# One more of the 16 states weighted on VectorE in half of the scan's tiles, and one product over two PSUM banks

## The chip, the cores and the metric

The kernel runs on one NeuronCore of a Trainium2 chip. The metric is the device time of one launch in microseconds. Before the change the median of three runs is 2026.62 us (2025.83 to 2028.26).

## The reference, cut to what matters

Input x is 4 sequences of 1024 tokens, 256 features, float32. Four stages follow one another, each added to x: latent attention, a spiking feed-forward layer, a selective scan, and the feed-forward layer again. The change is in the scan alone, which computes for each feature d and each of 16 states n:

```
A_tilde = exp(dt[..., None] * A)                    # A = -exp(A_log)
B_tilde = where(|A| < 1e-8, dt, (A_tilde - 1) / (A + 1e-10))
h   = A_t * h + B_t * Bp_t[:, None, :] * u_t[:, :, None]     # over time
y_t = einsum('bn,bdn->bd', Cp_t, h)
y = (y + u * D_param) * silu(z);   return y @ W_out.T
```

## The kernel before, in words

`scan` puts features on partitions (256 features are two halves, f = 0 and 1) and time on the free axis. Time is cut into 8 tiles of 512 tokens; a sequence is two tiles. Tiles 0, 2, 4 and 6 begin a sequence, so their recurrence starts from zero; tiles 1, 3, 5 and 7 take an incoming state. In each tile a loop over n = 0..15 takes one state at a time, "a unit" g = 16 t + n, all five engines in program order with semaphores between them; there is no scheduler, the order is the order of the code.

One unit goes through these steps:

- SyncE loads B and C of the state, spread over the partitions, into `bc` (L1556).
- GpSimd multiplies u by B into `ring` (`make_input`, L1574, 128x1024), three units ahead of the unit that it weighs next.
- ScalarE makes the decay exp(dt a) for each half in the PSUM pair `a_bank[g % 2]` (L1780). As there are two pairs, decay g waits until unit g-2 has left its pair: until it is scanned, and, if VectorE weighs unit g-2, until it has been weighed and its last column saved.
- VectorE forms (a - 1) x in `ring` (`scale`, L1895), then the recurrence (`run`, L1904), for each half.
- The result is multiplied by C ("weighted") into `outs`, 128x1024: on GpSimd (L1582) for most units, on VectorE (`weigh`, L1912) for the units that `on_dve` names. For those, the recurrence is written back into `a_bank` rather than `ring`.
- In tiles that begin a sequence ScalarE copies the last column into `state` (`keep_state`, L1794), right before decay g if unit g-2 is weighted on VectorE, right behind it otherwise.
- TensorE adds the unit into two PSUM banks `y_bank` with a diagonal matrix (L1639), three units late.

Work for other tiles is laid between the units. On ScalarE: at n = 6, 8, 9, 10, 11 and 12 pieces of the next tile's softplus and of its u (at n = 10 a table load, two logarithms and a second table load, L1756, L1759, L1741; at n = 8 and 12 a table load, silu and a table load), at n = 14 silu(z) of half 0 between two table loads (L1738, L1741), and half 1 at n = 0 of the next tile. On VectorE: `gate` (L1872) at n = 2 multiplies the previous tile's two y banks by silu(z), one 128x512 product each, a residual add at n = 3 and n = 15, and `soft`, three products, behind n = 11 and behind n = 12.

VectorE's order around a unit: scale(g, half 1), then weigh(g-1) if it is VectorE's, run(g, half 0), scale(g+1, half 0), run(g, half 1), then the extras of that n.

Of the kernel before, what the change touches and what calls it, by code (L numbers as in the profile page):

```python
# [6 lines left out]
F32 = mybir.dt.float32  # L7
BF16 = mybir.dt.bfloat16
I32 = mybir.dt.int32
ALU = mybir.AluOpType  # L10
# [3 lines left out]
P = 128  # L14
B, S, D = 4, 1024, 256
T = B * S
TW = 512
NT = T // TW
TPB = S // TW
DC = D // P  # L20
# [10 lines left out]
NS = 16  # L31
# [1433 lines left out]
def scan(nc, io, x, xn, xn_scr, w, begun, bc_scr, next_loads, xn_next):  # L1465
# [8 lines left out]
    OUTS = 5  # L1474
    AHEAD = 3
    LAG = 3
    D_UNIT = 8
    ON_DVE, ON_DVE_LAST = (3, 7, 11), (3, 6, 9, 12, 15)
    with ExitStack() as ctx:
        m = Mem(nc, ctx)  # L1480
        wz, wout, wtap, wpar, wdt, b_dt = (w[n] for n in ("wz", "wout", "wtap", "wpar", "wdt", "b_dt"))
        a_col, is_small = w["decay"][:, 1], w["decay"][:, 2]
        d_diag, rec_diag, ones, small_int, par, dt, bc = (begun[n] for n in (
            "d_diag", "rec_diag", "ones", "small_int", "par", "dt", "bc"))
        u = [begun["u0"], m.sb("u1", [P, DC, TW])]
        state = m.sb("state", [P, DC, NS])
        e_part, relu_part, log_part = (m.sb(n, [P, DC, TW]) for n in ("e_part", "relu_part", "log_part"))
        sz = m.sb("sz", [P, 2, DC, TW])
        gy = m.sb("gy", [P, DC, TW])
        ring = m.sb("ring", [P, RING, DC, TW])  # L1490
        outs = m.sb("outs", [P, OUTS, DC, TW])
        small_part = m.sb("small_part", [P, TW])
        norm = TokenNorm(m, x, w["ident"], "_nx", e_part[:].rearrange("p c (j d) -> p (c j) d", d=D))
        a_bank = [m.ctx.enter_context(nc.psum_tensor(f"a_bank{i}", [P, DC, TW], F32)) for i in range(2)]
        y_bank = [m.bank(f"ys_bank{f}") for f in range(DC)]
        w0, w1 = m.bank("work0"), m.bank("work1")

        decay_set, taps_set, diag_set, bc_out_done, bc_in = (begun[n] for n in (
# [22 lines left out]
            return (t + 1) // TPB * NS + (n if t % TPB == 0 else 0)  # L1521

        def on_dve(g):
            return g % NS in (ON_DVE if g // NS < NT - 1 else ON_DVE_LAST)

        def weighted_by(g):

            mine = on_dve(g)
            return (dve_weighted if mine else weighted), sum(on_dve(k) == mine for k in range(g + 1))
# [30 lines left out]
        def _(pool):  # L1560
# [26 lines left out]
            for g in range(UNITS):  # L1587
                if g + AHEAD < UNITS:
                    make_input(g + AHEAD)
                if not on_dve(g):  # L1590
                    weigh(g)

        @block.tensor
        def _(pe):
# [27 lines left out]
                product(bank, [(wz[:, c, f * P:(f + 1) * P], xn_of(t, c)) for c in range(DC)], z_made)  # L1622

            def out(t, i, bank):
                pe.wait_ge(gated, DC * t + DC)
                for b in (2 * i, 2 * i + 1):
                    for f in range(DC):
                        mm = nc.tensor.matmul(bank[:, b % 2 * D:(b % 2 + 1) * D], gy[:, f, b * P:(b + 1) * P], wout[:, f],
                                              start=(f == 0), stop=(f == DC - 1))
                mm.then_inc(out_made, 1)  # L1630

            def unit_sum(g):
                t, n = g // NS, g % NS
                if n == 0:

                    pe.wait_ge(gated, DC * t)
                pe.wait_ge(*weighted_by(g))
                for f in range(DC):
                    mm = nc.tensor.matmul(y_bank[f][:], rec_diag[:, f * NS + n], outs[:, g % OUTS, f],  # L1639
                                          start=(n == 0), stop=(n == NS - 1))  # L1640
                    if n == D_UNIT and f == 0:
                        for k in range(DC):
                            nc.tensor.matmul(y_bank[k][:], d_diag[:, k], u[t % 2][:, k], start=False, stop=False)
                mm.then_inc(summed, 1)

            pe.wait_ge(diag_set, 1)
# [2 lines left out]
            for t in range(NT):  # L1649
                more = t + 1 < NT  # L1650
                for n in range(NS):
                    if t >= TPB and n == 2:

                        pe.wait_ge(z_kept, DC * t)
                        out(t - 2, 1, w1)
# [37 lines left out]
                    if t and more and n == 15:  # L1693

                        pe.wait_ge(soft_made, DC * (t + 2))
                        out(t - 1, 0, w0)
                    if not more and n == 5:

                        pe.wait_ge(x_new, 2 * (t - 1))
                        out(t - 1, 0, w0)  # L1700
# [6 lines left out]
                    if t * NS + n >= LAG:  # L1707
                        unit_sum(t * NS + n - LAG)
            for g in range(UNITS - LAG, UNITS):
                unit_sum(g)  # L1710
# [5 lines left out]
        def _(act):  # L1716
# [16 lines left out]
            def silu_z(t, f, bank):  # L1733
                act.wait_ge(z_made, DC * t + f + 1)
                if t >= 2:

                    act.wait_ge(gated, DC * (t - 1))
                nc.scalar.activation(sz[:, t % 2, f], bank, ACT.Silu).then_inc(z_kept, 1)  # L1738

            def exp_tables():  # L1740
# [55 lines left out]
            for t in range(NT):  # L1796
                more = t + 1 < NT
                for n in range(NS):
                    g = t * NS + n
# [5 lines left out]
                    if t and n == 0:  # L1805
                        silu_z(t - 1, 1, w1[:])
                        exp_tables()
# [30 lines left out]
                    if n == 14:  # L1838
                        silu_z(t, 0, w1[:])
                        exp_tables()  # L1840
                    if not more and n == 15:
                        silu_z(t, 1, w1[:])
                        exp_tables()
# [4 lines left out]
        def _(dve):  # L1848
# [16 lines left out]
            def gate(t):  # L1865
                dve.wait_ge(summed, NS * t + NS)
                dve.wait_ge(z_kept, DC * t + DC)
                if t:

                    dve.wait_ge(out_made, DC * t)  # L1870
                for f in range(DC):
                    nc.vector.tensor_tensor(gy[:, f], y_bank[f][:], sz[:, t % 2, f], ALU.mult).then_inc(gated, 1)  # L1872

            def add(t, i, bank):
                dve.wait_ge(out_made, 2 * t + i + 1)
# [42 lines left out]
            def tiles(with_small):  # L1918
                scale(0, 0, with_small)
                for t in range(NT):  # L1920
                    more = t + 1 < NT
                    for n in range(NS):
                        g = t * NS + n
                        scale(g, 1, with_small)
                        if g and on_dve(g - 1):
                            weigh(g - 1)
                        run(g, 0)
                        if g + 1 < UNITS:
                            scale(g + 1, 0, with_small)
                        run(g, 1)  # L1930
                        if t and n == 2:
                            gate(t - 1)
                        if t >= TPB and n == 3:
                            add(t - 2, 1, w1)
                        if more and n == 11:
                            soft(t + 1, 0, w0[:])
                        if more and n == 12:
                            soft(t + 1, 1, w0[:])
                        if t and more and n == 15:
                            add(t - 1, 0, w0)  # L1940
                        if not more and n == 5:
                            add(t - 1, 0, w0)
                        if not more and n == 6:
                            add(t - 1, 1, w1)
                        if not more and n == 4:
                            norm.statistics(nc, dve, 0, 0)
                        if not more and n == 7:
                            norm.finish(nc, dve, 0)
# [5 lines left out]
            if on_dve(UNITS - 1):  # L1954
                weigh(UNITS - 1)
            gate(NT - 1)
            add(NT - 1, 0, w0)
            add(NT - 1, 1, w1)
# [35 lines left out]
def program(nc, io, out):  # L1994
# [5 lines left out]
    with ExitStack() as ctx:  # L2000
# [8 lines left out]
        with ExitStack() as second:  # L2009
            m = Mem(nc, second)  # L2010
            xn_scan = m.sb("xn_s", [P, XN, DC, TAPS - 1 + TW])
            w, loads = scan_weights(m, io)
            wpr_last = m.sb("wpr_f2", [P, FC, D])
            ident = w["ident"]
            with ExitStack() as feed:
                given = feed_weights(Mem(nc, feed), io, "_f1")
                merge_heads(nc, io, x, o_scr, recip_scr, early, given[2], ident, given[3])
                merging.close()
                begun = first_scan_tile(m)
                feed_forward(nc, x, "_f1", given[:3], ident, io=io, xn_scan=xn_scan, xn_scr=xn_scr, more_loads=loads, w=w,  # L2020
                             begun=begun, bc_scr=bc_scr)
            wfc_last = w["wtap"][:].rearrange("p k c d -> p (k c d)").rearrange("p (c f) -> p c f", c=DC)

            def xn_next(c):
                return xn_scan[:, (NT + 1) % XN, c, 0:TW]

            scan(nc, io, x, xn_scan, xn_scr, w, begun, bc_scr,
                 ((wfc_last, io["W_fcT"].rearrange("(c p) f -> p c f", p=P)),
                  (wpr_last[:], io["W_projT"].rearrange("(f p) d -> p f d", p=P))), xn_next)
            xn_last = m.sb("xn_f2", [P, 2, DC, TW])  # L2030
            feed_forward(nc, x, "_f2", (wfc_last, wpr_last, xn_last), ident, out=out, xn_first=xn_next)
# [13 lines left out]
```

## Time and profile before

| what | value |
|---|---|
| median of three runs | 2026.62 us |
| the profiled execution | 2029.69 us, span 2027.7 us |
| TensorE granted clock, mean | 0.957 |
| busy, share of the span | PE 92%, DVE 80%, ACT 54%, POOL 34% |
| the scan, VectorE's first to last instruction | about 1240.7 to 1792.9 us of the span |

PE is TensorE, DVE VectorE, ACT ScalarE, POOL GpSimd, SP SyncE; PEld is TensorE's weight load. The shares of the whole span mix four stages, so the scan has to be read from its own stretch. A row of the trace gives start, duration, engine, line, operation, and in brackets how long that engine sat idle before it and what ended the wait. Durations of neighbouring VectorE rows overlap by about 0.1 us; start-to-start distances are what an instruction costs.

### The profile page before, as it was taken

What the parts mean: (1) busy time and instruction counts of PE and PEld (TensorE: products, weight loads), DVE (VectorE), ACT (ScalarE), POOL (GpSimd) and SP (SyncE); (2) the same over time, 40 slices, a digit from 0 to 9 for tenths busy, and PEclk for the clock granted to TensorE, in tenths of its full rate; (3) what the DMA queues carried; (4) which work ended last, traced back from release to release, by engine and by line L of the source; (5) the groups of instructions that cost most, each with busy time, mean ns of one, the idle gap of its engine ahead of it and who ended that gap; (6) DMA issues with size and microseconds to landing.
All of it is one profiled execution on the core that took longest, in us unless ns stands there. A gap on an engine that the chain in (4) does not pass through costs nothing. (4 is left out here: it accounts for less than half of the span.)

```text
span 2027.7 us, 25794 instructions
## 1 busy us (share of the span) xinstructions
PE 1868.1 (92%) x7414; PEld 826.8 (41%) x7414; DVE 1625.9 (80%) x2596; ACT 1087.7 (54%) x1511; POOL 697.9 (34%) x474
## 2 busy tenths in 40 slices
PE   7898999999999999999999997798889877789998
PEld 4441332332322322323676663333333333356665
DVE  6878998998998988974556666999999999955654
ACT  5552665666665666674244335766576657333321
POOL 3561000001100000010000015999999999800000
PEclk9996998999998999999999997899999999899999
DMA  4850222122221122203210003455545545400000
GB/s 134 175 129 13 62 51 42 45 43 44 46 45 44 43 48 38 48 12 122 82 42 21 22 23 118 126 143 136 135 121 142 137 122 164 99 6 16 22 21 21
DMA packets 100394, 147.13 MB, mean 73 GB/s; under 512 B 15089, under 2 KB 54401, under 8 KB 98721
## 3 DMA queue, kind: packets, MB, share of 16 engines
q1 hardware_dynamic: 100256, 145.42, 28.6%
q8 instruction: 72, 1.18, 0.3%
q14 instruction: 66, 0.53, 0.1%
HBM read 114.69 MB, written 30.29 MB: 71 GB/s over the span
## 5 line engine op out<-in xcount | busy, mean ns | idle before, releaser
L840 DVE TENSOR_REDUCE mx<-max_bank 128x1 f32<-128x512 f32 x960 | 618.1, 687 | 65.0 <-PE max_bank L749 64.7
L826 ACT ACTIVATE probs<-score_bank 128x1024 f32<-128x1024 f32 x512 | 496.9, 1021 | 289.7 <-PE score_bank L763 288.8
L749 PE MATMUL max_bank<-ks,qs 96*128 96x512 bf16 x960 | 336.0, 390 | 0.0
L763 PE MATMUL score_bank<-qs,ks 99*128 99x512 bf16 x1024 | 313.6, 388 | 14.5 <-issue 10.4
L1639 PE MATMUL ys_bank<-outs,rec_diag 128*128 128x512 f32 x512 | 260.2, 642 | 67.3 <-POOL outs L1582 43.5
L1574 POOL TENSOR_TENSOR ring<-u,bc 128x1024 f32<-128x1024 f32 x128 | 300.6, 2359 | 0.4 <-DMA bc<-bc_scr 0.3
L809 PE MATMUL o_bank<-probs,vg 128*32 128x512 f32 x2048 | 275.5, 610 | 0.5 <-ACT probs L826 0.5
L1780 ACT ACTIVATE a_bank<-dt,decay_s 128x512 f32<-128x512 f32 x256 | 170.7, 686 | 150.5 <-DVE ring L1904 98.1
L1582 POOL TENSOR_TENSOR outs<-ring,bc 128x1024 f32<-128x1024 f32 x102 | 239.9, 2352 | 13.6 <-DVE ring L1904 13.6
L1252 PE MATMUL y_bank_f<-wpr_f,hid_f 128*128 128x256 f32 x1024 | 236.4, 379 | 0.0
L703 POOL CAST neg_parts<-neg_max 16x128 bf16<-16x128 f32 x31 | 8.7, 282 | 639.1 <-DVE neg_max L853 639.1
L1252 PEld LDWEIGHTS y_bank_f<-wpr_f,hid_f 128*128 128x128 f32 x1024 | 193.4, 190 | 59.9 <-issue 38.3
L1324 ACT ACTIVATE relu_f<-hid_bank_f 128x512 f32<-128x512 f32 x128 | 76.3, 596 | 250.9 <-PE hid_bank_f L1243 225.3
L749 PEld LDWEIGHTS max_bank<-ks,qs 96*128 96x128 bf16 x960 | 94.1, 98 | 281.1 <-DVE mx L840 187.1
L1895 DVE SCALAR_TENSOR_TENSOR ring<-a_bank,ring 128x512 f32<-128x512 f32 x256 | 172.6, 674 | 22.5 <-ACT a_bank L1780 21.6
L1639 PEld LDWEIGHTS ys_bank<-outs,rec_diag 128*128 128x128 f32 x512 | 99.3, 202 | 207.6 <-issue 114.9
L1414 DVE SCALAR_TENSOR_TENSOR hid_f<-hid_bank_f,relu_f 128x512 f32<-128x512 f32 x128 | 86.9, 688 | 97.0 <-ACT relu_f L1324 95.2
L763 PEld LDWEIGHTS score_bank<-qs,ks 99*128 99x128 bf16 x1024 | 99.6, 100 | 123.1 <-issue 27.4
L1904 DVE TENSOR_TENSOR_SCAN ring<-a_bank,state,ring 128x512 f32<-128x512 f32 x100 | 127.8, 1278 | 0.0
L1904 DVE TENSOR_TENSOR_SCAN ring<-a_bank,ring 128x512 f32<-128x512 f32 x104 | 126.3, 1214 | 0.0
L1243 PE MATMUL hid_bank_f<-xn_f,wfc_f 128*128 128x512 f32 x256 | 116.5, 592 | 1.1 <-PEq L972 1.1
L1613 PE MATMUL work<-xn_s,wtap_s 128*128 128x512 f32 x224 | 107.0, 616 | 7.3 <-DVE x L1876 7.3
(233 smaller groups left out, 1933.7 us busy)
## 6 DMA issues: line engine op xcount, KB each, us to landing
bc<-bc_scr SPq DMA_DIRECT2D x128, 512.0 KB, 5.0
qk_parts<-parts SPq DMA_DIRECT2D x128, 96.0 KB, 1.9
qs<-qk_parts SPq DMA_DIRECT2D x128, 64.0 KB, 4.3
o_scr<-o_sb SPq DMA_DIRECT2D x32, 256.0 KB, 2.0
ks<-qk_parts SPq DMA_DIRECT2D x16, 384.0 KB, 4.7
xn_s<-xn_scr SPq DMA_DIRECT2D x8, 515.0 KB, 6.3
x<-in_x_dram SPq DMA_DIRECT2D x8, 512.0 KB, 4.3
ks<-qk_parts SPq DMA_DIRECT2D x16, 256.0 KB, 3.5
```

What stands on the lines that cost most here:

```text
L749: nc.tensor.matmul(max_bank[(r + a) % MB][:], qs[r][0:SROWS, half, j, qt * P:(qt + 1) * P], ks[r][0:SROWS, j, kh * TW:(kh + 1) * TW], star ...
L763: mm = nc.tensor.matmul(score_bank[pair][:, j % 2], ks[r][0:MROWS, j, kt * P:(kt + 1) * P], qs[r][0:MROWS, qh, j, :], start=True, stop=True)
L809: mm = nc.tensor.matmul(o_bank[32 * j:32 * j + 32, :], vg[r][:, kt, j], probs[:, s % 2, j], start=(kt == 0), stop=(kt == QT - 1))
L826: nc.scalar.activation(probs[:, s % 2, 2 * pair:2 * pair + 2], score_bank[pair][:], ACT.Exp, scale=SOFTMAX_SCALE).then_inc(probs_ready, 1)
L840: nc.vector.tensor_reduce(mx[:, a // HU, a % HU:a % HU + 1], max_bank[(r + a) % MB][:], AX_X, ALU.max)\
L1252: mm = nc.tensor.matmul(y_of(b), hid[:, f, b * P:(b + 1) * P], wpr[:, f], start=(f == 0), stop=(f == FC - 1))
L1574: nc.gpsimd.tensor_tensor(ring[:, g % RING], u[t % 2][:], bc[:, g % BC, 0:1].to_broadcast([P, DC, TW]), ALU.mult).then_inc(inputs, 1)
L1582: nc.gpsimd.tensor_tensor(outs[:, g % OUTS], ring[:, g % RING], bc[:, g % BC, 1:2].to_broadcast([P, DC, TW]), ALU.mult).then_inc(weighted, 1)
L1639: mm = nc.tensor.matmul(y_bank[f][:], rec_diag[:, f * NS + n], outs[:, g % OUTS, f], start=(n == 0), stop=(n == NS - 1))
L1780: nc.scalar.activation(a_bank[g % 2][:, f], dt[:, t % 2, f], ACT.Exp, scale=a_col[:, f, n:n + 1])\
L1895: nc.vector.scalar_tensor_tensor(x, a, 1.0, x, ALU.subtract, ALU.mult).then_inc(scaled, 1)
L1904: nc.vector.tensor_tensor_scan(a if on_dve(g) else x, a, x, state[:, f, n:n + 1] if t % TPB else 0.0, ALU.mult, ALU.add)\
```

## The change

Three units per tile are weighted on VectorE before, n = 3, 7 and 11 (five in the last tile). After, the tiles that begin a sequence (0, 2, 4, 6) have four, n = 2, 5, 8 and 12; the others keep theirs. The product with silu(z) becomes one 128x1024 operation over a PSUM tensor of two banks, and its semaphore counts once a tile rather than twice.

```diff
-    ON_DVE, ON_DVE_LAST = (3, 7, 11), (3, 6, 9, 12, 15)
+    ON_DVE, ON_DVE_FIRST, ON_DVE_LAST = (3, 7, 11), (2, 5, 8, 12), (3, 6, 9, 12, 15)
...
-        y_bank = [m.bank(f"ys_bank{f}") for f in range(DC)]
+        y_banks = m.ctx.enter_context(nc.psum_tensor("ys_banks", [P, DC, TW], F32))
+        y_bank = [y_banks[:, f] for f in range(DC)]
...
         def on_dve(g):
-            return g % NS in (ON_DVE if g // NS < NT - 1 else ON_DVE_LAST)
+            if g // NS == NT - 1:
+                return g % NS in ON_DVE_LAST
+            return g % NS in (ON_DVE if g // NS % TPB else ON_DVE_FIRST)
...
-                for f in range(DC):
-                    nc.vector.tensor_tensor(gy[:, f], y_bank[f][:], sz[:, t % 2, f], ALU.mult).then_inc(gated, 1)
+                nc.vector.tensor_tensor(gy[:], y_banks[:], sz[:, t % 2], ALU.mult).then_inc(gated, 1)
...
-                pe.wait_ge(gated, DC * t + DC)
+                pe.wait_ge(gated, t + 1)
```

The other waits on `gated` are counted down in the same way.

ScalarE in tile 2, from the save of the last column or the decay ahead of the logarithms. Before, the pair of decays behind `state<-a_bank1` is unit 9's, and the wait for VectorE's weighted unit 7 stands there:

```order
L1794 ACTIVATE state<-a_bank1 128x2
L1780 ACTIVATE a_bank1<-dt,decay_s 128x512 x2
L1748 ACTIVATE e_part<-work0,b_dt_s 128x512
L1749 ACTIVATE relu_part<-work0,b_dt_s 128x512
L1753 ACTIVATE e_part<-e_part 128x512 x2
L1780 ACTIVATE a_bank0<-dt,decay_s 128x512 x2
L1794 ACTIVATE state<-ring 128x2
L1756 ACT_TABLE_LOAD
L1759 ACTIVATE log_part<-e_part,ones 128x512 x2
L1741 ACT_TABLE_LOAD
L1780 ACTIVATE a_bank1<-dt,decay_s 128x512 x2
```

The same place after the change (lines are 3 higher). `state<-a_bank0` is unit 8's:

```order
L1783 ACTIVATE a_bank1<-dt,decay_s 128x512 x2
L1797 ACTIVATE state<-ring 128x2
L1751 ACTIVATE e_part<-work0,b_dt_s 128x512
L1752 ACTIVATE relu_part<-work0,b_dt_s 128x512
L1756 ACTIVATE e_part<-e_part 128x512 x2
L1797 ACTIVATE state<-a_bank0 128x2
L1783 ACTIVATE a_bank0<-dt,decay_s 128x512 x2
L1759 ACT_TABLE_LOAD
L1762 ACTIVATE log_part<-e_part,ones 128x512 x2
L1744 ACT_TABLE_LOAD
L1783 ACTIVATE a_bank1<-dt,decay_s 128x512 x2
```

The save and its wait moved from ahead of unit 9's decay to ahead of unit 10's, directly in front of the logarithms.

ScalarE in tile 2 around silu(z) of half 0, before. `state<-a_bank1` is unit 11's and waits for its weighting; the last row is unit 15's decay:

```order
L1766 ACTIVATE work0<-e_part,ones 128x512
L1794 ACTIVATE state<-a_bank1 128x2
L1780 ACTIVATE a_bank1<-dt,decay_s 128x512 x2
L1780 ACTIVATE a_bank0<-dt,decay_s 128x512 x2
L1794 ACTIVATE state<-ring 128x2
L1738 ACT_TABLE_LOAD
L1738 ACTIVATE sz<-work1 128x512
L1741 ACT_TABLE_LOAD
L1780 ACTIVATE a_bank1<-dt,decay_s 128x512 x2
```

And after. `state<-a_bank0` is unit 12's:

```order
L1769 ACTIVATE work0<-e_part,ones 128x512
L1783 ACTIVATE a_bank1<-dt,decay_s 128x512 x2
L1797 ACTIVATE state<-ring 128x2
L1797 ACTIVATE state<-a_bank0 128x2
L1783 ACTIVATE a_bank0<-dt,decay_s 128x512 x2
L1741 ACT_TABLE_LOAD
L1741 ACTIVATE sz<-work1 128x512
L1744 ACT_TABLE_LOAD
L1783 ACTIVATE a_bank1<-dt,decay_s 128x512 x2
```

The wait moved from ahead of unit 13's decay to ahead of unit 14's, one decay pair in front of silu(z) and its two table loads.

VectorE in tile 0 from `soft` behind n = 11 (the first L1854 row), before. The weighting of unit 11 (L1912) stands between two `soft` groups:

```order
L1854 SCALAR_TENSOR_TENSOR work0<-work0,e_part 128x512
L1858 TENSOR_TENSOR work0<-log_part,work0 128x512
L1863 TENSOR_TENSOR dt<-work0,relu_part 128x512
L1895 SCALAR_TENSOR_TENSOR ring<-a_bank0,ring 128x512
L1912 TENSOR_TENSOR outs<-a_bank1,bc 128x1024
L1904 SCALAR_TENSOR_TENSOR ring<-a_bank0,ring 128x512
L1895 SCALAR_TENSOR_TENSOR ring<-a_bank1,ring 128x512
L1904 SCALAR_TENSOR_TENSOR ring<-a_bank0,ring 128x512
L1854 SCALAR_TENSOR_TENSOR work0<-work0,e_part 128x512
```

After, from the same place on. The weighting is unit 12's and stands behind the second `soft` group:

```order
L1906 SCALAR_TENSOR_TENSOR a_bank0<-a_bank0,ring 128x512
L1857 SCALAR_TENSOR_TENSOR work0<-work0,e_part 128x512
L1861 TENSOR_TENSOR work0<-log_part,work0 128x512
L1866 TENSOR_TENSOR dt<-work0,relu_part 128x512
L1897 SCALAR_TENSOR_TENSOR ring<-a_bank1,ring 128x512
L1914 TENSOR_TENSOR outs<-a_bank0,bc 128x1024
L1906 SCALAR_TENSOR_TENSOR ring<-a_bank1,ring 128x512
L1897 SCALAR_TENSOR_TENSOR ring<-a_bank0,ring 128x512
```

The weighting moved one unit later, behind the second `soft` group.

## Rows read from the trace of the kernel before

**Rows 1.** Page, costliest groups: GpSimd's two products, VectorE's wait for decays.
```profile
L1574 POOL TENSOR_TENSOR ring<-u,bc 128x1024 f32<-128x1024 f32 x128 | 300.6, 2359 | 0.4 <-DMA bc<-bc_scr 0.3
L1582 POOL TENSOR_TENSOR outs<-ring,bc 128x1024 f32<-128x1024 f32 x102 | 239.9, 2352 | 13.6 <-DVE ring L1904 13.6
L1895 DVE SCALAR_TENSOR_TENSOR ring<-a_bank,ring 128x512 f32<-128x512 f32 x256 | 172.6, 674 | 22.5 <-ACT a_bank L1780 21.6 <-POOL ring L1574 0.8
```
**Rows 2.** Busy time of each engine over tile 4.
```profile
core 0: us, PE busy (x) PEld busy (x) DVE busy (x) ACT busy (x) POOL busy (x), PEclk, DMA share, GB/s
1509.97:1577.02 67.05, 58.24 (x133) 25.72 (x132) 64.92 (x79) 44.65 (x73) 66.82 (x30) 0.95 0.51 134
```
**Rows 3.** Timeline of GpSimd, tile 4, near its end.
```profile
1569.15 2.35 POOL L1582 TENSOR_TENSOR outs<-ring,bc 128x1024 f32<-128x1024 f32 x1 [0.23 <-DVE ring L1904]
1571.46 2.35 POOL L1574 TENSOR_TENSOR ring<-u,bc 128x1024 f32<-128x1024 f32 x1
```
**Rows 4.** Timeline of VectorE: every wait of tiles 0, 2, 4, 6 after the start.
```profile
1276.70 0.69 DVE L1895 SCALAR_TENSOR_TENSOR ring<-a_bank,ring 128x512 f32<-128x512 f32 x1 [0.31 <-POOL ring L1574]
1281.65 0.69 DVE L1895 SCALAR_TENSOR_TENSOR ring<-a_bank,ring 128x512 f32<-128x512 f32 x1 [1.42 <-ACT a_bank L1780]
...
1399.23 0.69 DVE L1895 SCALAR_TENSOR_TENSOR ring<-a_bank,ring 128x512 f32<-128x512 f32 x1 [0.36 <-ACT a_bank L1780]
...
1416.09 0.69 DVE L1895 SCALAR_TENSOR_TENSOR ring<-a_bank,ring 128x512 f32<-128x512 f32 x1 [1.81 <-ACT a_bank L1780]
...
1551.50 0.69 DVE L1895 SCALAR_TENSOR_TENSOR ring<-a_bank,ring 128x512 f32<-128x512 f32 x1 [1.85 <-ACT a_bank L1780]
...
1686.66 0.69 DVE L1895 SCALAR_TENSOR_TENSOR ring<-a_bank,ring 128x512 f32<-128x512 f32 x1 [1.84 <-ACT a_bank L1780]
```
**Rows 5.** Timeline of VectorE, tile 0, around the weighting of unit 3.
```profile
1251.59 0.67 DVE L1895 SCALAR_TENSOR_TENSOR ring<-a_bank,ring 128x512 f32<-128x512 f32 x1
...
1255.02 0.68 DVE L1895 SCALAR_TENSOR_TENSOR ring<-a_bank,ring 128x512 f32<-128x512 f32 x1
1255.61 1.21 DVE L1912 TENSOR_TENSOR outs<-a_bank,bc 128x1024 f32<-128x1024 f32 x1
1256.74 1.22 DVE L1904 TENSOR_TENSOR_SCAN ring<-a_bank,ring 128x512 f32<-128x512 f32 x1
1257.93 0.69 DVE L1895 SCALAR_TENSOR_TENSOR ring<-a_bank,ring 128x512 f32<-128x512 f32 x1
...
1259.67 0.67 DVE L1895 SCALAR_TENSOR_TENSOR ring<-a_bank,ring 128x512 f32<-128x512 f32 x1
...
1261.38 0.67 DVE L1895 SCALAR_TENSOR_TENSOR ring<-a_bank,ring 128x512 f32<-128x512 f32 x1
```
**Rows 6.** Timeline of ScalarE, tile 0: decays behind a weighting, logarithms, silu(z).
```profile
1257.21 1.91 ACT L1780 ACTIVATE a_bank<-dt,decay_s 128x512 f32<-128x512 f32 x3
...
1276.99 1.28 ACT L1756 ACT_TABLE_LOAD   x1
...
1280.93 1.30 ACT L1780 ACTIVATE a_bank<-dt,decay_s 128x512 f32<-128x512 f32 x2
...
1294.54 1.28 ACT L1738 ACT_TABLE_LOAD   x1
1295.84 0.60 ACT L1738 ACTIVATE sz<-work 128x512 f32<-128x512 f32 x1
...
1297.75 0.69 ACT L1780 ACTIVATE a_bank<-dt,decay_s 128x512 f32<-128x512 f32 x1
```
**Rows 7.** Timeline of VectorE, tile 1, the product with silu(z).
```profile
1316.63 1.27 DVE L1872 TENSOR_TENSOR gy<-ys_bank,sz 128x512 f32<-128x512 f32 x2
1317.81 0.69 DVE L1895 SCALAR_TENSOR_TENSOR ring<-a_bank,ring 128x512 f32<-128x512 f32 x1
```
**Rows 8.** VectorE's product with silu(z), all 16: its wait for TensorE.
```profile
L1872 DVE TENSOR_TENSOR gy<-ys_bank,sz 128x512 f32<-128x512 f32 x16 | 10.2, 680 | 2.1 <-PE ys_bank L1639 2.1
```
**Rows 9.** Timeline of GpSimd and of VectorE in the last tile.
```profile
1746.95 2.34 POOL L1582 TENSOR_TENSOR outs<-ring,bc 128x1024 f32<-128x1024 f32 x1 [0.67 <-DVE ring L1904]
...
1746.96 2.35 DVE L932 SCALAR_TENSOR_TENSOR step_nx<-step_nx,guess_rs_nx 128x4 f32<-128x4 f32 x1
```

More of the change, by code:

```diff
@@ L1634, in unit_sum @@
                 if n == 0:
-                    pe.wait_ge(gated, DC * t)
+                    pe.wait_ge(gated, t)
                 pe.wait_ge(*weighted_by(g))
                 for f in range(DC):
-                    mm = nc.tensor.matmul(y_bank[f][:], rec_diag[:, f * NS + n], outs[:, g % OUTS, f],
+                    mm = nc.tensor.matmul(y_bank[f], rec_diag[:, f * NS + n], outs[:, g % OUTS, f],
                                           start=(n == 0), stop=(n == NS - 1))
@@ L1642, in unit_sum @@
                         for k in range(DC):
-                            nc.tensor.matmul(y_bank[k][:], d_diag[:, k], u[t % 2][:, k], start=False, stop=False)
+                            nc.tensor.matmul(y_bank[k], d_diag[:, k], u[t % 2][:, k], start=False, stop=False)
                 mm.then_inc(summed, 1)
@@ L1735, in silu_z @@
                 if t >= 2:
-                    act.wait_ge(gated, DC * (t - 1))
+                    act.wait_ge(gated, t - 1)
                 nc.scalar.activation(sz[:, t % 2, f], bank, ACT.Silu).then_inc(z_kept, 1)
```

## The prediction

> **What bounds the kernel now.** The diff touches the scan alone, so I left the chain that ended last aside: it lies in the final feed-forward stage and names no line of the scan. I read the list of costliest groups first. It shows two engines that could set the scan's pace: GpSimd with 128 inputs and 102 weightings of 2.36 and 2.35 us, and VectorE. The reader should look at the idle columns. GpSimd waited 13.6 us for VectorE's recurrence; VectorE waited 21.6 us for decays of ScalarE and only 0.8 us for GpSimd's inputs [rows 1]. The busy times of one tile come next: in tile 4, 67.05 us long, GpSimd is busy 66.82 us and VectorE 64.92 us [rows 2]. By share alone GpSimd looks like the bound. So the timelines have to decide, and they say VectorE. Near the end of tile 4 GpSimd waits 0.23 us for a recurrence, thus it had caught up with VectorE [rows 3]; in tiles 0, 2, 4 and 6 VectorE waits once for GpSimd (0.31 us, tile 0) and otherwise for ScalarE: 1.42 us in tile 0, 0.36 and 1.81 in tile 2, 1.85 in tile 4, 1.84 in tile 6 [rows 4]. VectorE's instructions stand back to back elsewhere. Its own time, plus what ScalarE makes it wait, is the tile's length. The balance is close, though: GpSimd's 29 products at a start-to-start distance of 2.31 us [rows 3] are 67.0 us, as long as the tile.
>
> **Part 1, the extra weighting on VectorE.** Four tiles get one more. From scale to scale of the next unit takes 1255.02 - 1251.59 = 3.43 us without a weighting and 1259.67 - 1255.02 = 4.65 us with one [rows 5], so one costs 1.22 us: 1.13 for its own slot, the rest lost by the decay that waits for it. Nothing hides it, since it stands in the queue that sets the pace. 4 x 1.22 = +4.9 us.
>
> What it takes off GpSimd is 2.31 us per tile, but GpSimd is the engine that waits. I cost this at nothing, except that VectorE's 0.31 us in tile 0 goes (counted in part 2). TensorE, SyncE's loads of bc and the ring's slots wait for weightings too, and each gets them no later than before.
>
> **Part 2, where the weightings stand.** This costs as much as part 1. ScalarE may not write a pair of decay banks until VectorE has weighed what is in it. Call W the end of a weighting. Unit 3's ends at 1255.61 + 1.21 = 1256.82; the decay pair that waited for it starts at 1257.21 = W + 0.39 [rows 5, 6], and a pair without a third behind it takes 1.30 us, so ScalarE is free at W + 1.70 (a table load starts 0.02 us later at most). VectorE, where nothing holds it, comes to the scale of two units on at 1261.38 = W + 4.56 [rows 5]. A scale starts 1281.65 - 1280.93 = 0.72 us after its decay starts [rows 4, 6].
>
> *Logarithms.* The weighting of unit 8 now gates unit 10's decay, and the logarithm block stands directly behind that pair. It takes 1280.93 - 1276.99 = 3.94 us with its two table loads [rows 6]. Unit 11's decay starts at W + 5.64, its scale at W + 6.36, and VectorE wants it at W + 4.56: a wait of 1.80 us. Softplus's split and exponentials at n = 9 now run ahead of W, while ScalarE waits anyhow. Before, in the same place, unit 7's weighting two units earlier held the whole queue, and VectorE waited 1.42 + 0.31, 1.81 + 0.36, 1.85 and 1.84 us, 7.6 in four tiles [rows 4]. After it is 4 x 1.80 = 7.2. Change -0.4 us.
>
> *silu(z).* Before, unit 11's weighting gated unit 13's decay, and silu(z) with its two table loads came a pair later, with room; no wait of VectorE stands in [rows 4] after 1281.65 in tile 0. Now unit 12's weighting gates unit 14's decay and silu(z) is right behind. It takes 1297.75 - 1294.54 = 3.21 us [rows 6]. Unit 15's decay starts at W + 1.70 + 3.21 = W + 4.91, its scale at W + 5.63, and VectorE wants it at W + 4.56: a new wait of 1.07 us, 4 x 1.07 = +4.3 us.
>
> The weightings of units 2 and 5 gate the decays of 4 and 7. Behind unit 4's stands one 96x512 copy. Behind unit 7's stands unit 8's, then silu(u) at n = 8, with 3.4 us more of VectorE's work before unit 9 is wanted. I compute a margin of about 0.3 us there and count nothing; if it fails it is a few tenths in each of four tiles.
>
> The trace shows no silu(z) wait of this kind, so its bounds: from below 0, if ScalarE has slack that I overlook; from above the largest wait of the rows behind such a block, 1.85 us a tile [rows 4], 7.4 in all. I take 4.3 because the same steps give 1.80 for the logarithm block, near its measured 1.8.
>
> The Trainium skill has a rule on these blocks ("ScalarE: Activation LUTs", section "What ACT_TABLE_LOAD costs"): a switch of tables costs a load of 1283 ns plus a drain of about 1380 ns. The trace has the load at 1.28 us and the next ScalarE instruction 0.02 us behind it [rows 6]: no such drain is seen. By the page as an estimate, two switches in each silu(z) block would add 2.8 us a tile, 11 us in all; by the rows they add nothing.
>
> **Part 3, one product over both banks.** The two products take 1317.81 - 1316.63 = 1.18 us to the next start [rows 7]; an operation of the same size and operand places, the weighting, takes 1256.74 - 1255.61 = 1.13 us [rows 5]. That is 0.05 us in eight tiles, -0.4 us. Bounds: 0, and 0.1 a tile.
>
> The Trainium skill ("Perfetto Trace Analysis", section "Optimizing Scalar/DVE Operations") gives about 125 ns of overhead per VectorE instruction on PSUM, which would make the saving 1.0 us as an estimate; the rows show less than half, so they decide.
>
> TensorE waits for both halves before and after, so the joint semaphore delays nobody. In the tiles with the new wait silu(z) ends later, so TensorE's z product of half 1 and the last sums come later too; the product with silu(z) waited for TensorE only 2.1 us, all in the final tile [rows 8], and it stands more than two units behind. I count nothing.
>
> **Sum.** 4.9 - 0.4 + 4.3 - 0.4 = +8.4 us. Tiles 1, 3, 5 and 7 keep their order and are left as they are. The profiled execution goes from 2029.69 to 2038.1 us. The median of the runs is 3.1 us below the profiled execution, and the same sum on it gives 2026.62 + 8.4 = 2035.0 us. What a measurement can tell from no change is 0.2%, 4.1 us.
>
> **Rivals.**
>
> *A, the sum above*: 2035.0 us. Chance 0.62.
>
> *B, the silu(z) wait stays hidden.* ScalarE would have to reach silu(z) earlier than W + 1.70, or VectorE be late by other waits. For it: no row shows the wait; ScalarE is busy only 44.65 of 67.05 us [rows 2]. Against: that is an average, and the order in the program puts the block right behind the gated pair. Then 4.9 - 0.4 - 0.4 = +4.1, 2030.7 us. Chance 0.16.
>
> *C, GpSimd paces these tiles.* The point from which this decides: VectorE's waits for ScalarE must be there only because GpSimd's lateness reaches ScalarE through TensorE (the sums wait for weightings, the softplus products stand behind the sums). The 0.36 us of tile 2 looks like that. Then with 28 products GpSimd needs 28 x 2.31 = 64.7 us, the waits fall away, and the tile is VectorE's own: 67.05 - 1.85 + 1.22 = 66.4 us, 0.6 less than now; four tiles and part 3 give -3.0, 2023.6 us, not slower than before. For it: 29 x 2.31 is 67.0, just the tile's length. Against: GpSimd waits for VectorE in the same tile [rows 3], and the blocks of ScalarE account for the waits. Chance 0.09.
>
> *D, the added work meets GpSimd's port.* In the last tile a VectorE operation on 128x4 elements takes 2.35 us beside a GpSimd product that started 0.01 us before and takes 2.34 [rows 9], so a VectorE instruction can be held through one. If each added weighting were held for half of one, 1.2 us, four cost 4.7 more: 2039.7 us. Against: the weighting of unit 3 started on time among GpSimd's back-to-back products and took 1.21 us [rows 5]. Chance 0.04. The Trainium skill ("SBUF — State Buffer", section "SBUF: two separate sides") names this an exclusive lock, taken by a VectorE operation with two SBUF inputs against a GpSimd one; the held operation has two, the weighting has one operand in PSUM, and the trace agrees.
>
> *E, late chains*: unit 9's margin fails, or TensorE's late sums reach the product with silu(z). Some 0.5 to 1 us a tile more, about 2038 us. Chance 0.09.
>
> **How the numbers follow.** A's own range, with part 2 and 3 within a few tenths per tile and the runs' own 1 us, is 2032.5 to 2037.5. B, half of D and most of E have to be inside for 8 in 10: 2029.5 to 2038.5, which leaves out C (0.09), D and the edges. Slower by more than 0.2% (above 2030.7): A, D, E and half of B, 0.83. Faster by more than 0.2% (below 2022.6): only the far side of C, 0.03. Within: 0.14.
>
> **What would show it.** The tile lengths from first scale to first scale: 69 to 69.5 us for tiles 2, 4 and 6 rather than 67 to 67.5. VectorE's waits for decays: about 1.8 us at unit 11 and about 1.1 us at unit 15 in each of the four tiles. GpSimd's wait for recurrences up from 13.6 by some 15 us or more, since it has 9 us less to do and 8 us more time. One row of silu(z)'s product, 128x1024, x8. Wrong would be: tiles 0, 2, 4, 6 shorter than 67 us, a wait of VectorE for GpSimd's inputs, or a weighting that takes over 1.3 us.

## The result, and the profile after

Beside the changed kernel the kernel before was timed again. The changed kernel takes 2039.85 us (median of five, 2035.26 to 2040.21), the kernel before 2028.26 us (median of five, 2025.83 to 2029.98). The ratio is 1.0048, with a 95% interval of 1.0037 to 1.0059: slower, by 7.5 to 12.0 us, 9.7 at its centre. The forecast was 2035.0 us, slower by 8.4, with a range of 2029.5 to 2038.5. It was built on the earlier median of the kernel before, 2026.62 us; times the ratio, that gives 2036.3 us, inside the range. The median of 2039.85 us as it stands lies 1.3 us above the range; the kernel before, too, took 1.6 us longer this time than when the forecast was made.

The profiled execution went from 2029.69 to 2035.76 us, 6.1 us, where the medians differ by 11.6. Of the five executions of the changed kernel two took 2035.3 and 2035.8 us and three 2039.9 to 2040.2; the profiled one is of the first kind, and no trace shows what the others spent their 4 us on. From the first recurrence of tile 0 to the start of the last product with silu(z) the scan takes 545.1 us before and 554.3 after, +9.1 us, and what lies around it 1482.6 and 1479.2 us. The code around it is the same. In the ten profiles of this study that part varies between 1474 and 1483 us, so tile lengths are compared below; they do not contain it.

| us, from first recurrence to first recurrence | t0 | t1 | t2 | t3 | t4 | t5 | t6 | t7 |
|---|---|---|---|---|---|---|---|---|
| before | 64.68 | 67.52 | 67.51 | 68.36 | 67.05 | 68.11 | 67.04 | 74.86 |
| after | 66.98 | 67.46 | 69.17 | 68.30 | 69.91 | 68.06 | 69.17 | 75.22 |

(Tile 7 ends where the last product with silu(z) starts.) The four tiles with a fourth weighting grew by 2.30, 1.66, 2.86 and 2.13 us, the others hardly moved.

The page of after, the groups that answer to [rows 1]:

```profile
L1577 POOL TENSOR_TENSOR ring<-u,bc 128x1024 f32<-128x1024 f32 x128 | 300.9, 2363 | 0.0
L1585 POOL TENSOR_TENSOR outs<-ring,bc 128x1024 f32<-128x1024 f32 x98 | 231.1, 2358 | 31.8 <-DVE ring L1906 31.6
...
L1897 DVE SCALAR_TENSOR_TENSOR ring<-a_bank,ring 128x512 f32<-128x512 f32 x256 | 171.8, 671 | 26.9 <-ACT a_bank L1783 16.8
```

GpSimd has 98 weightings instead of 102 and its wait for VectorE's recurrences went from 13.6 to 31.6 us. What was taken off it became idle time. VectorE's wait went from 22.5 to 26.9 us, but its releasers can't be compared row by row: 9.89 us of it is the start of the scan, booked to another releaser than the 9.66 us of before. Behind the start VectorE waited 12.8 us before and 17.0 after, and each wait has to be looked up.

The timeline of VectorE after, all waits of tiles 0, 2, 4 and 6 behind the start, against [rows 4]:

```profile
1279.61 0.69 DVE L1897 SCALAR_TENSOR_TENSOR ring<-a_bank,ring 128x512 f32<-128x512 f32 x1 [1.73 <-ACT a_bank L1783]
1299.89 0.69 DVE L1897 SCALAR_TENSOR_TENSOR ring<-a_bank,ring 128x512 f32<-128x512 f32 x1 [0.99 <-ACT a_bank L1783]
...
1415.65 0.69 DVE L1897 SCALAR_TENSOR_TENSOR ring<-a_bank,ring 128x512 f32<-128x512 f32 x1 [1.73 <-ACT a_bank L1783]
1435.92 0.69 DVE L1897 SCALAR_TENSOR_TENSOR ring<-a_bank,ring 128x512 f32<-128x512 f32 x1 [0.99 <-ACT a_bank L1783]
...
1537.11 0.69 DVE L1897 SCALAR_TENSOR_TENSOR ring<-a_bank,ring 128x512 f32<-128x512 f32 x1 [0.71 <-ACT a_bank L1783]
1553.86 0.69 DVE L1897 SCALAR_TENSOR_TENSOR ring<-a_bank,ring 128x512 f32<-128x512 f32 x1 [1.73 <-ACT a_bank L1783]
1574.13 0.69 DVE L1897 SCALAR_TENSOR_TENSOR ring<-a_bank,ring 128x512 f32<-128x512 f32 x1 [0.99 <-ACT a_bank L1783]
...
1691.09 0.69 DVE L1897 SCALAR_TENSOR_TENSOR ring<-a_bank,ring 128x512 f32<-128x512 f32 x1 [1.73 <-ACT a_bank L1783]
1711.36 0.69 DVE L1897 SCALAR_TENSOR_TENSOR ring<-a_bank,ring 128x512 f32<-128x512 f32 x1 [0.99 <-ACT a_bank L1783]
```

The wait of 1.73 us is unit 11's, behind the logarithms; 0.99 us is unit 15's, behind silu(z), and is new in all four tiles. One more stands in tile 4 alone, 0.71 us at unit 7. GpSimd's inputs are waited for nowhere.

The chain of the new wait, on ScalarE and on VectorE in tile 0 after:

```profile
1294.36 0.17 ACT L1797 ACTIVATE state<-a_bank 128x2 f32<-128x2 f32 x1 [5.25 <-DVE outs L1914]
1294.65 1.30 ACT L1783 ACTIVATE a_bank<-dt,decay_s 128x512 f32<-128x512 f32 x2
1295.96 1.28 ACT L1741 ACT_TABLE_LOAD   x1
1297.26 0.60 ACT L1741 ACTIVATE sz<-work 128x512 f32<-128x512 f32 x1
1297.87 1.28 ACT L1744 ACT_TABLE_LOAD   x1
1299.17 1.30 ACT L1783 ACTIVATE a_bank<-dt,decay_s 128x512 f32<-128x512 f32 x2
```

```profile
1293.05 1.22 DVE L1914 TENSOR_TENSOR outs<-a_bank,bc 128x1024 f32<-128x1024 f32 x1
1294.18 1.21 DVE L1906 TENSOR_TENSOR_SCAN ring<-a_bank,ring 128x512 f32<-128x512 f32 x1
...
1297.69 1.21 DVE L1906 TENSOR_TENSOR_SCAN ring<-a_bank,ring 128x512 f32<-128x512 f32 x1
```

ScalarE sat idle for 5.25 us until VectorE's weighting of unit 12 ended at 1294.27, and only then did unit 14's decays, silu(z) and its two table loads come, 4.5 us in a row. VectorE ran out of work at 1298.9 and went on at 1299.89.

### The profile page after: what moved, and what is told of

Read it like the earlier page. It is cut to its first block and busy times, and to the rows that moved or that the text cites. A ratio compares the mean times of both kernels' runs of the same rounds, so it can differ in the third digit from the quotient of the medians.

```text
span 2033.5 us, 25795 instructions
## 1 busy us (share of the span) xinstructions
PE 1866.5 (92%) x7414; PEld 830.6 (41%) x7414; DVE 1630.5 (80%) x2592; ACT 1087.2 (53%) x1511; POOL 688.8 (34%) x470
## 5 line engine op out<-in xcount | busy, mean ns | idle before, releaser
L1642 PE MATMUL ys_banks<-outs,rec_diag 128*128 128x512 f32 x512 | 252.3, 628 | 54.3 <-POOL outs L1585 26.7
L1585 POOL TENSOR_TENSOR outs<-ring,bc 128x1024 f32<-128x1024 f32 x98 | 231.1, 2358 | 31.8 <-DVE ring L1906 31.6
L1897 DVE SCALAR_TENSOR_TENSOR ring<-a_bank,ring 128x512 f32<-128x512 f32 x256 | 171.8, 671 | 26.9 <-ACT a_bank L1783 16.8
L1642 PEld LDWEIGHTS ys_banks<-outs,rec_diag 128*128 128x128 f32 x512 | 99.5, 199 | 187.3 <-issue 122.1
L1906 DVE TENSOR_TENSOR_SCAN ring<-a_bank,ring 128x512 f32<-128x512 f32 x96 | 116.4, 1213 | 0.0
```

The costliest lines, as they stand in the source:

```text
L1585: nc.gpsimd.tensor_tensor(outs[:, g % OUTS], ring[:, g % RING], bc[:, g % BC, 1:2].to_broadcast([P, DC, TW]), ALU.mult).then_inc(weighted, 1)
L1642: mm = nc.tensor.matmul(y_bank[f], rec_diag[:, f * NS + n], outs[:, g % OUTS, f], start=(n == 0), stop=(n == NS - 1))
L1897: nc.vector.scalar_tensor_tensor(x, a, 1.0, x, ALU.subtract, ALU.mult).then_inc(scaled, 1)
L1906: nc.vector.tensor_tensor_scan(a if on_dve(g) else x, a, x, state[:, f, n:n + 1] if t % TPB else 0.0, ALU.mult, ALU.add)\
```

## The experiments

All variants but two are the changed kernel with one edit; of the two others one edits the kernel before and one is the kernel before itself. The last tile keeps its five weightings in all of them. Ratios are to the kernel before, with 95% intervals.

**The one product alone.**

```diff
-ON_DVE, ON_DVE_FIRST, ON_DVE_LAST = (3, 7, 11), (2, 5, 8, 12), (3, 6, 9, 12, 15)
+ON_DVE, ON_DVE_FIRST, ON_DVE_LAST = (3, 7, 11), (3, 7, 11), (3, 6, 9, 12, 15)
```

> The changed kernel with the weightings put back to 3, 7 and 11 in all tiles but the last; what is left of the change is the one product with silu(z). Theory (VectorE paces the scan): 0.05 us less per product, 0.4 us in all, within noise of the kernel before; tiles 4 and 6 take 67.0 us, VectorE waits 1.8 us at unit 11 of tiles 0, 2, 4, 6 and not at unit 15. Rival (the merged product or its joint semaphore costs something of the measured 0.48%): 2 us or more slower than the kernel before, and a wait of VectorE near n = 2.

Measured: ratio 0.9998 (0.9989 to 1.0008). The one product takes 1199 ns instead of two of 680, and its only wait, 3.8 us for TensorE, is in the last tile:

```profile
L1874 DVE TENSOR_TENSOR gy<-ys_banks,sz 128x1024 f32<-128x1024 f32 x8 | 9.6, 1199 | 3.8 <-PE ys_banks L1642 3.8
```

The interval ends at 1.6 us slower, so the product can't account for the 0.48%, and its gain of 0.4 us can't be seen in the total. Two misses: tiles 4 and 6 take 67.46 and 67.76 us, not 67.0, because 0.37 and 0.68 us of waiting at unit 7 came up; the last experiment is on that.

**The fourth weighting one unit earlier.**

```diff
-ON_DVE, ON_DVE_FIRST, ON_DVE_LAST = (3, 7, 11), (2, 5, 8, 12), (3, 6, 9, 12, 15)
+ON_DVE, ON_DVE_FIRST, ON_DVE_LAST = (3, 7, 11), (2, 5, 8, 11), (3, 6, 9, 12, 15)
```

> The changed kernel with the fourth weighting at n = 11 instead of 12 in tiles 0, 2, 4, 6; four weightings, one unit earlier. Theory (a weighting one decay pair ahead of the silu(z) block causes the wait at unit 15): that wait of 0.99 us goes in all four tiles, the one at unit 11 stays at 1.73, tile 6 takes 68.2 us against 69.17, and the kernel is about 4 us faster than the changed one and 5 slower than before. Rival (the wait comes with the fourth weighting wherever it stands, since ScalarE falls behind by load): tile 6 stays at 69.2 us.

Measured: ratio 1.0031 (1.0022 to 1.0041). The timeline of VectorE has two waits in tile 6 and none at unit 15:

```profile
1674.64 0.69 DVE L1897 SCALAR_TENSOR_TENSOR ring<-a_bank,ring 128x512 f32<-128x512 f32 x1 [0.50 <-ACT a_bank L1783]
1691.39 0.69 DVE L1897 SCALAR_TENSOR_TENSOR ring<-a_bank,ring 128x512 f32<-128x512 f32 x1 [1.73 <-ACT a_bank L1783]
```

The wait of 0.99 us is gone in all four tiles with the same four weightings, so it does not come with their number. Tile 6 takes 68.60 us, where 68.2 was expected: less the 0.50 at unit 7, which the changed kernel did not have there, 68.10. Tiles 2 and 4 have larger waits at unit 7, 1.93 and 1.16 us, and take 70.03 and 69.27 us, 68.10 and 68.11 without them. So of the 4 us that the move gains this profile shows only 1.6 in the scan, 552.7 us against 554.3; the ratios differ by 3.5 us.

**Three weightings in the late positions.**

```diff
-ON_DVE, ON_DVE_FIRST, ON_DVE_LAST = (3, 7, 11), (2, 5, 8, 12), (3, 6, 9, 12, 15)
+ON_DVE, ON_DVE_FIRST, ON_DVE_LAST = (3, 7, 11), (3, 8, 12), (3, 6, 9, 12, 15)
```

> The changed kernel with three weightings, n = 3, 8 and 12, in tiles 0, 2, 4, 6: the count of before, the late positions of after. Theory (each weighting costs 1.22 us, positions cost by themselves): waits of 1.73 us at unit 11 and 0.99 at unit 15, tile 6 takes 67.95 us, the scan is some 3.5 us longer than before, 0.2%. Rival (only the count matters, or GpSimd's 29 products of 2.31 us set the pace): tile 6 takes 67.0 us and the time is that of before.

Measured: ratio 1.0017 (1.0007 to 1.0026). The timeline of VectorE in tile 6:

```profile
1669.68 0.69 DVE L1897 SCALAR_TENSOR_TENSOR ring<-a_bank,ring 128x512 f32<-128x512 f32 x1 [0.47 <-ACT a_bank L1783]
1686.42 0.69 DVE L1897 SCALAR_TENSOR_TENSOR ring<-a_bank,ring 128x512 f32<-128x512 f32 x1 [1.73 <-ACT a_bank L1783]
1706.69 0.69 DVE L1897 SCALAR_TENSOR_TENSOR ring<-a_bank,ring 128x512 f32<-128x512 f32 x1 [0.99 <-ACT a_bank L1783]
```

With the count of before, position alone brings both waits, 1.73 and 0.99 us. Tile 6 takes 68.52 us, 68.05 without the wait at unit 7, where 67.95 was expected; against the changed kernel's 69.17 the fourth weighting then costs 1.1 us (1.22, 1.11 and 1.15 in tiles 0, 2 and 4, reckoned alike). Count and position are two separate costs.

**Less work for GpSimd, none more for VectorE.** On the kernel before; units 5 and 13 are weighted for half of the features only, so part of the sum over states is left out. The branch for all other units is as it was.

```diff
+if g // NS < NT - 1 and g // NS % TPB == 0 and g % NS in (5, 13):
+    nc.gpsimd.tensor_tensor(outs[:, g % OUTS, 0:1], ring[:, g % RING, 0:1],
+                            bc[:, g % BC, 1:2], ALU.mult).then_inc(weighted, 1)
+else:
...
```

> The kernel before, with GpSimd's weightings of units 5 and 13 in tiles 0, 2, 4, 6 cut to the first half of the features (the second half of the output is left as it was, so part of the sum over states is not computed). GpSimd has 2.3 us less to do per tile, VectorE nothing more. Theory (VectorE paces): tiles 4 and 6 stay at 67.05 us, only tile 0 loses the 0.3 us wait for an input, and GpSimd's wait for recurrences grows by 8 to 9 us. Rival (GpSimd paces these tiles, directly or through late sums on TensorE): tiles of 66.0 to 66.5 us and the kernel 2 to 4 us faster.

Measured: ratio 0.9995 (0.9984 to 1.0005). Tiles 4 and 6 take 67.04 and 67.04 us against 67.05 and 67.04, with the same wait for ScalarE:

```profile
1545.08 0.69 DVE L1899 SCALAR_TENSOR_TENSOR ring<-a_bank,ring 128x512 f32<-128x512 f32 x1 [1.84 <-ACT a_bank L1784]
...
1680.24 0.69 DVE L1899 SCALAR_TENSOR_TENSOR ring<-a_bank,ring 128x512 f32<-128x512 f32 x1 [1.85 <-ACT a_bank L1784]
```

Most of the 2.3 us a tile turned into GpSimd's idle time: its wait for recurrences is 18.2 + 3.4 = 21.6 us instead of 13.6, up 8.0:

```profile
L1586 POOL TENSOR_TENSOR outs<-ring,bc 128x1024 f32<-128x1024 f32 x94 | 221.4, 2355 | 18.2 <-DVE ring L1908 18.2
L1583 POOL TENSOR_TENSOR outs<-ring,bc 128x512 f32<-128x512 f32 x8 | 10.1, 1266 | 3.4 <-DVE ring L1908 3.4
```

GpSimd, busy 66.82 of 67.05 us [rows 2], paced nothing there. In tile 0 the expected 0.3 us did not come: the wait for the input went, the one for ScalarE grew from 1.42 to 1.84, and the tile stayed at 64.67. ScalarE was late there by about as much. Tile 2 went from 67.51 to 67.04 us; that is not GpSimd's doing, since the second profile of the kernel before, below, has it at 67.05.

**silu(z) one unit earlier, the weightings of the change.**

```diff
-if n == 14:
+if n == (14 if t % TPB else 13):
     silu_z(t, 0, w1[:])
     exp_tables()
```

> The changed kernel (weightings 2, 5, 8, 12) with ScalarE's silu(z) of half 0 laid behind unit 13's decay instead of unit 14's in tiles 0, 2, 4, 6; nothing else moves. Theory (the wait at unit 15 comes from the block standing behind the decay that waits for unit 12's weighting): the block now runs while ScalarE would wait, the 0.99 us at unit 15 goes, 1.73 us at unit 11 stays, and tile 6 takes 68.2 us. Rival (ScalarE is late there by its load, or the z product of TensorE is late): the wait at unit 15 stays at 0.5 us or more.

Measured: ratio 1.0019 (1.0008 to 1.0030). The timeline of ScalarE in tile 4 shows the block (the table load, silu(z), the second table load) ahead of the wait for unit 12's weighting:

```profile
1565.87 1.28 ACT L1741 ACT_TABLE_LOAD   x1
1567.16 0.60 ACT L1741 ACTIVATE sz<-work 128x512 f32<-128x512 f32 x1
1567.77 1.28 ACT L1744 ACT_TABLE_LOAD   x1
1571.09 0.17 ACT L1797 ACTIVATE state<-a_bank 128x2 f32<-128x2 f32 x1 [2.03 <-issue]
```

No wait stands at unit 15 in any of the four tiles. Tile 2, without a wait at unit 7, takes 68.07 us; tiles 4 and 6 take 69.91 and 69.08 with 1.81 and 0.97 us at unit 7, so the length of 68.2 is met there only once that is taken off. With ScalarE's order alone, and VectorE's and GpSimd's work as in the change, the new wait is undone.

**Weightings that gate no block.**

```diff
-ON_DVE, ON_DVE_FIRST, ON_DVE_LAST = (3, 7, 11), (2, 5, 8, 12), (3, 6, 9, 12, 15)
+ON_DVE, ON_DVE_FIRST, ON_DVE_LAST = (3, 9, 13), (3, 9, 13), (3, 6, 9, 12, 15)
```

> Three weightings in every tile but the last, at n = 3, 9 and 13, so that none gates the decay in front of the logarithms or of silu(z). Theory: in tiles 1, 3, 5 the wait of 1.21 us at unit 11 goes, 67.1 us a tile against 68.1; in tiles 0, 2, 4, 6 ScalarE makes VectorE wait 1.1 us at unit 11 instead of 1.85, but GpSimd's 29 products then set 67.0 us, so waits for its inputs appear and little is won. The scan is 3 to 4 us shorter than before, about 2023.5 us. Rival (ScalarE's blocks cost VectorE the same wherever the weightings stand): 1.2 to 1.85 us stays at unit 11 and the time is that of before.

Measured: ratio 0.9978 (0.9967 to 0.9988), faster than before by 2.4 to 6.7 us. VectorE's waits in tiles 0 and 1:

```profile
1268.13 0.69 DVE L1897 SCALAR_TENSOR_TENSOR ring<-a_bank,ring 128x512 f32<-128x512 f32 x1 [1.09 <-POOL ring L1577]
1277.38 0.69 DVE L1897 SCALAR_TENSOR_TENSOR ring<-a_bank,ring 128x512 f32<-128x512 f32 x1 [1.07 <-POOL ring L1577]
...
1335.13 0.69 DVE L1897 SCALAR_TENSOR_TENSOR ring<-a_bank,ring 128x512 f32<-128x512 f32 x1 [0.77 <-POOL ring L1577]
1344.38 0.69 DVE L1897 SCALAR_TENSOR_TENSOR ring<-a_bank,ring 128x512 f32<-128x512 f32 x1 [0.91 <-POOL ring L1577]
```

Tile 3 has no wait at all and takes 66.92 us (68.36 before). As most of ScalarE's waits went (the one at unit 11 is 1.0 us in tile 2, 0.5 in tile 4, 0.9 in tile 6), GpSimd became the late one: 4.6 us of waits for its inputs, which the kernel before had 0.8 of. Tiles 0 and 1, with two such waits each, got longer than before, 65.33 and 68.05 us. With these positions GpSimd has become a bound in some tiles, and taking work off it may pay, which the next version tries. One reserve: tiles 0 to 6 together are 2.1 us shorter than before, less than the 3 to 4 expected, and the last tile, where no position was changed, is 1.3 us longer than in the first profile of before, so the two profiled scans differ by 0.8 us only (544.3 and 545.1).

**Four weightings, none of which gates a block.**

```diff
-ON_DVE, ON_DVE_FIRST, ON_DVE_LAST = (3, 7, 11), (2, 5, 8, 12), (3, 6, 9, 12, 15)
+ON_DVE, ON_DVE_FIRST, ON_DVE_LAST = (3, 9, 13), (1, 5, 9, 13), (3, 6, 9, 12, 15)
```

> Four weightings in tiles 0, 2, 4, 6 at n = 1, 5, 9 and 13, three in the others at 3, 9 and 13. Theory: each added weighting costs VectorE 1.22 us, the wait at unit 11 is 1.1 us and none stands at unit 15, so tiles 2, 4, 6 take 67.5 us, 1.7 less than the changed kernel; the others 67.1. The scan is 1 to 2 us shorter than before, some 2 us longer than with 3, 9 and 13 everywhere. Rival (a fourth weighting costs the whole 69 us): tile 6 over 68.5 us.

Measured: 2023.98 us median, ratio 0.9968 (0.9954 to 0.9982), faster than before by 3.7 to 9.3 us. Its group of VectorE's scales, where `issue` is the start of the scan, shows 5.4 us of waits for ScalarE and 0.9 for GpSimd:

```profile
L1897 DVE SCALAR_TENSOR_TENSOR ring<-a_bank,ring 128x512 f32<-128x512 f32 x256 | 172.0, 672 | 16.2 <-issue 9.8 <-ACT a_bank L1783 5.4 <-POOL ring L1577 0.9
```

and VectorE's only waits in tiles 0, 2 and 4, all at unit 11:

```profile
1279.39 0.69 DVE L1897 SCALAR_TENSOR_TENSOR ring<-a_bank,ring 128x512 f32<-128x512 f32 x1 [0.86 <-ACT a_bank L1783]
...
1413.34 0.69 DVE L1897 SCALAR_TENSOR_TENSOR ring<-a_bank,ring 128x512 f32<-128x512 f32 x1 [0.86 <-ACT a_bank L1783]
...
1547.29 0.69 DVE L1897 SCALAR_TENSOR_TENSOR ring<-a_bank,ring 128x512 f32<-128x512 f32 x1 [0.85 <-ACT a_bank L1783]
```

Tiles 2, 4 and 6 take 67.14, 67.14 and 67.63 us, 67.5 expected, against 69.17, 69.91 and 69.17 in the change: the same number of weightings on VectorE, 1.5 to 2.8 us less. The scan takes 542.6 us, 2.5 less than before. The intervals of this version and of 3, 9, 13 overlap, so which of the two is the better one is open; both beat the kernel before and the changed one. The expectation had this one's scan some 2 us longer than that of 3, 9, 13; it came out 1.7 us shorter, 1.4 us of that in the last tile, where the two do not differ.

**The kernel before, once more.**

> The kernel before, unchanged, for a second profile. Small waits of 0.3 to 1.9 us at unit 7 came up in the kernels with the one product, and 0.36 us once in the kernel before. Theory (they come from TensorE's granted clock, which differs from execution to execution): waits at unit 7 in some tiles here too, and tile lengths that differ from the first profile by 0.3 to 1 us where TensorE's clock is at its low level behind the product with silu(z). Rival (they come with the one product over both banks): no wait at unit 7 beyond 0.36 us.

One execution, no ratio. Waits at unit 7 stand in tiles 5 and 6, 0.20 and 0.59 us, and tile 6 takes 67.75 us instead of 67.04. The last product with silu(z) waits 3.76 us for TensorE instead of 2.08. The scan takes 547.2 us, 2.0 more than in the first profile, so a difference of two profiled scans is uncertain by about that much: after against before is +9.1 us by the first and +7.1 by the second. TensorE's timeline, tile 6, the products behind the residual add, in the first profile of before and in the second:

```profile
1660.18 3.70 PE L1613 MATMUL work<-xn_s,wtap_s 128*128 128x512 f32 x8 [0.36 <-DVE x L1876]
```

```profile
1654.13 5.63 PE L1613 MATMUL work<-xn_s,wtap_s 128*128 128x512 f32 x8 [1.33 <-DVE x L1876]
```

And busy times over just these stretches, first and second profile, PEclk being the granted clock as a share of 2.4 GHz (the first row names the columns, and PEclk is the third number from the end):

```profile
core 0: us, PE busy (x) PEld busy (x) DVE busy (x) ACT busy (x) POOL busy (x), PEclk, DMA share, GB/s
1660.18:1663.90 3.72, 3.72 (x9) 1.79 (x10) 3.72 (x5) 1.85 (x4) 3.72 (x2) 1.00 0.52 95
```

```profile
1654.13:1659.80 5.67, 5.67 (x9) 2.60 (x10) 5.67 (x7) 2.90 (x6) 5.67 (x3) 0.65 0.62 119
```

The same eight rows take 3.70 us at 2.4 GHz throughout, and 5.63 where the clock lay at 1.2 GHz for part of the stretch. TensorE had waited for the add in both, 0.36 and 1.33 us. The program is the same, so these waits are not the one product's. All ten profiles point the same way. Of their 50 tiles from 2 to 6, 21 have this stretch at 5.2 us or more, and 18 of those have a wait at unit 7; the other 29 have it at 4.7 us or less, and none has one. No run changed the clock by itself, so that it is the cause is read from this coincidence and not shown by an experiment.

## Why the prediction was right, step by step

- *VectorE paces the scan, GpSimd does not.* Shown: less work for GpSimd left tiles 4 and 6 at 67.04 us. Rival C had as its condition that ScalarE's waits were GpSimd's lateness in disguise; they stayed at 1.84 and 1.85 us. It falls for these weightings; only with 3, 9, 13 is GpSimd a bound, and there directly, through its inputs.
- *An added weighting costs 1.22 us.* 1.1 to 1.2 us a tile in the difference between the three-weighting variant and the change, 4.6 in four tiles, against 4.9.
- *The wait at unit 15, 1.07 us a tile.* 0.99 in each. The profile counts a wait from the end of the row before, and rows overlap; from start to start the wait costs 1299.89 - 1297.69 - 1.13 = 1.07 us, what was forecast (1.13 us is that distance where nothing waits). Position alone brings it, moving the weighting or the block alone takes it away: shown from three sides. Rival B falls.
- *The wait at unit 11, 1.80 us.* 1.73 in each, and 1.81 from start to start (2.94 - 1.13). The term itself was mis-sized: it set 1.80, reckoned from start to start, against 7.6 us of waits as the profile counts them. Counted alike before and after it is -0.7 (6.9 against 7.6) rather than -0.4 us.
- *One product for two, -0.05 us a tile.* Tiles 3 and 5 shortened by 0.05 to 0.06 us. The total can't show it.
- *Rival D, GpSimd's port.* All 30 weightings on VectorE after take 1.21 or 1.22 us, as before; none was held.
- *Rival E.* Waits of its kind stand in the profile: 0.71 us at unit 7 in tile 4, and 0.43 us more before the last product with silu(z) (2.51 against [rows 8]). That the change brings them is not shown, since the second profile of the kernel before has 0.20, 0.59 and 3.76 us in such places. I had put the margin at risk at unit 9; in the four tiles no wait came there, but at unit 7, where TensorE's clock was low. In tile 4 of after the products behind the add ran at a granted clock of 0.68:

```profile
1526.74:1532.14 5.40, 5.40 (x9) 2.37 (x10) 5.40 (x7) 1.73 (x5) 5.40 (x3) 0.68 0.80 239
```

and ScalarE, which waited 3.97 us for what TensorE makes behind them, reached unit 7's decay late. In tile 3, before and after, the same stretch took 5.40 us too, and VectorE did not wait.

The signs named ahead came: the waits in all four tiles, GpSimd's wait for recurrences up by 18 us, one row for the product, x8, and 69.2 us from first scale to first scale for tiles 2 and 6. Tile 4 took 70.0 by its 0.71 us.

The sum again with measured terms: 4.6 for the weightings, 4 x 0.99 = 4.0 for unit 15, -0.7 for unit 11, 0.7 for unit 7, 0.4 in the last tile, -0.4 for the products: 8.6 of the scan's 9.1 us. The terms for unit 7 and the last tile, 1.1 us, were not in the forecast, and the others came out 0.9 lower than forecast. So that 8.4 lies so near the measured difference is in part luck, while the mechanism and its two main terms are shown. The ratio's centre, 9.7 us, is above the sum, its interval holds it.

## What to carry to other kernels

Of two engines that are both busy for nearly the whole tile, ask which one waits for the other. Here GpSimd did, busy 66.8 of 67.05 us, and cutting its work by 2.3 us a tile gained nothing. The balance can turn: with the weightings at 3, 9 and 13 VectorE waited for GpSimd. When work is handed to the pacing engine its position counts as much as its amount: ask which buffer it keeps, who waits for that buffer, and what stands right behind that waiting instruction in its queue. A long block should come ahead of the gated instruction, where it runs during the wait, or the gating work be moved a step away: unit 11 or 13 instead of 12 removed the wait at unit 15.

## What the runs showed that I had not expected

- An added VectorE weighting can cost nothing where GpSimd was late. In tile 0 the version with four (1, 5, 9, 13) takes 64.84 us, the one with three (3, 9, 13) 65.33, because GpSimd is then in time with its inputs (waits of 1.09 and 1.07 us against none). It is not so everywhere: in tiles 4 and 6, where GpSimd's lateness was small or nil, the version with four takes 0.6 and 1.4 us more.
- TensorE, which waits for others in every tile, can still delay the scan when its clock is low. In tile 4 of the silu(z) variant the eight rows behind the add took 6.50 us at a granted clock of 0.56 and VectorE lost 1.81 us at unit 7; in the changed kernel they took 5.40 us at 0.68, and it lost 0.71; in tile 6 of the first profile of before 3.70 us at 1.00, and it lost nothing. One program shows it in one execution and not in the next. The cause is read from the profiles, as said above.
- Tiny operations can be long: the 128x4 operation of [rows 9] ended with the GpSimd product beside it. No experiment was made on it.
